# A mixture-of-experts FFN turned round on one Trainium2 core: weights stationary, each expert's 320 lanes moving, tokens scattered to regions in DRAM

## What is computed

```python
x = x + xattn(_layernorm(x), ctx_1024, ctx_1024, Wq, bq, Wk, bk, Wv, bv)
xt = _layernorm(x).reshape(-1, 128)                     # 1024 tokens
top_vals, top_idx = jax.lax.top_k(xt @ gate_w.T, 2)
top_w = jax.nn.softmax(top_vals, axis=-1)
combine = jnp.einsum('tke,tk->te', jax.nn.one_hot(top_idx, 8), top_w)
h = jax.nn.silu(jnp.einsum('td,ehd->eth', xt, w1)) * jnp.einsum('td,ehd->eth', xt, w3)
ye = jnp.einsum('eth,edh->etd', h, w2)                  # w1, w3: 8 x 512 x 128, w2: 8 x 128 x 512
x = x + jnp.einsum('te,etd->td', combine, ye)
```

## Time and profile before

| | us |
|---|---|
| median of three runs | 136.7 |
| lowest and highest | 135.67, 137.67 |
| span of the profiled execution | 132.1 |
| PE busy, POOL busy | 102.9, 84.8 |
| DVE busy, ACT busy | 78.5, 44.1 |

### The profile page before, as it was taken

How to read it: one execution, slowest core, us unless ns; L and a number is a source line. 1 busy time by engine, 2 the same in 40 slices (tenths; PEclk the granted TensorE clock), 3 DMA queues, 4 the chain that set the end, 5 groups by cost and what they waited for, 6 DMA issues and landing times. The chain is left out here.

```text
span 132.1 us, 2609 instructions
## 1 busy us (share of the span) xinstructions
PE 102.9 (78%) x571; PEld 71.5 (54%) x571; DVE 78.5 (59%) x276; ACT 44.1 (33%) x109; POOL 84.8 (64%) x122
## 2 busy tenths in 40 slices
PE   6869976789899279998977897997897979993000
PEld 2245962525355057886866675765675756762000
DVE  0862589897897969996745554563465545632000
ACT  4035877647700013343242033333234033331000
POOL 3387008383975926498769968969979697573630
PEclk9999999869599955999999999999999999999855
DMA  3969999500130002032232322202222323222220
GB/s 108 264 250 424 424 429 404 171 6 0 48 113 18 23 9 39 0 45 24 36 45 40 40 32 27 40 20 40 40 40 40 36 24 40 36 24 20 20 20 0
DMA packets 8119, 11.42 MB, mean 86 GB/s; under 512 B 880, under 2 KB 6896, under 8 KB 7344
## 3 DMA queue, kind: packets, MB, share of 16 engines
q1 hardware_dynamic: 4592, 8.70, 17.7%
q0 software_dynamic: 3520, 2.64, 15.6%
HBM read 8.91 MB, written 2.43 MB: 86 GB/s over the span
## 5 line engine op out<-in xcount | busy, mean ns | idle before, releaser
L381 POOL DMA_INDIRECT out_rows<-y_sb,aid x20 | 31.9, 1595 | 13.9 <-SPq L290 6.4
L523 ACT ACTIVATE hidT<-bank 128x256 f32<-128x256 f32 x40 | 13.5, 382 | 45.6 <-PE bank L997 37.6
L1007 PEld LDWEIGHTS bank<-w_sb,hidT 128*128 128x128 f32 x160 | 19.6, 191 | 7.6 <-issue 7.0
L1007 PE MATMUL bank<-w_sb,hidT 128*128 x160 | 22.4, 283 | 1.6 <-ACT hidT L523 0.9
L360 POOL DMA_INDIRECT xg<-tok_rows,gid x18 | 18.4, 1020 | 7.5 <-DVE slot_w L764 3.4
L974 PE MATMUL bank<-w_hi,xgT 128*128 x40 | 20.1, 503 | 3.0 <-DVE xgT L756 3.0
L910 PE MATMUL bank<-ones 128*128 128x512 bf16 x66 | 20.5, 463 | 1.1 <-DVE ones L544 1.1
L516 ACT ACTIVATE sil<-bank 128x512 f32<-128x512 f32 x20 | 12.1, 603 | 13.9 <-PE bank L976 12.1
L773 DVE TENSOR_TENSOR hid<-bank,sil 128x512 f32<-128x512 f32 x20 | 13.8, 690 | 4.6 <-PE bank L976 2.6
L975 PE MATMUL bank<-w_lo,xgT 128*128 x40 | 16.5, 413 | 0.0
L976 PE MATMUL bank<-w_hi,xgT 128*128 x40 | 16.5, 412 | 0.0
(11 more groups left out here) (120 smaller groups left out, 144.3 us busy)
## 6 DMA issues: line engine op xcount, KB each, us to landing
w_sb<-in_w1T SPq DMA_DIRECT2D x2, 1024.0 KB, 9.9
w_sb<-in_w3T SPq DMA_DIRECT2D x2, 1024.0 KB, 13.6
w_sb<-in_w2T SPq DMA_DIRECT2D x2, 1024.0 KB, 17.2
tok_rows<-tok SPq DMA_DIRECT2D x1, 520.0 KB, 4.4
x_sb<-in_x SPq DMA_DIRECT2D x2, 256.0 KB, 3.2
out_rows<-x SPq DMA_DIRECT2D x2, 256.0 KB, 4.7
ctxT_sb<-in_ctxT SPq DMA_DIRECT2D x1, 480.0 KB, 5.1
out_rows<-y_sb,aid POOLq DMA_INDIRECT x20
```

The costliest lines, as they stand in the source:

```text
L381: nc.gpsimd.indirect_dma_start(out[:, :], bass.IndirectOffsetOnAxis(ap=aid[p][:, 0:1], axis=0), y_sb[p][:, :], None, compute_op=ALU.add).t ...
L523: nc.scalar.activation(hidT[p][:, h * H // 2:(h + 1) * H // 2], ps_hT[h][:, 0:H // 2], ACT.Copy).then_inc(s_hidT, 1)
L1007: last = mm(ps_y[:, 0:D], hidT[p][:, c * P:(c + 1) * P], w2_sb[:, bass.ds(e * H + c * D, D)], start=(c == 0), stop=(c == HC - 1))
```

## The change

**Routing.** Each expert has a region of 1088 rows in a DRAM tensor `expert_rows`; the first 320 (`CAP`) are used by the main part. SP fills these 320 rows of all experts with zeros and row numbers of spare rows, by 16 transfers that stand between w3 and w2 in its queue. The rank product gets the region's start added (`region`), so that the product and sum in `slots` give the row of each pair directly. A row carries the 128 numbers, the token's row in `out` and the weight of the pair; `tok` is there twice, once for each choice (`twin_rows` on ACT). POOL scatters it with 16 indexed DMAs (one for each of 8 batches and 2 choices), and SP loads the regions back, two loads for each expert. The tables of tiles, one-hots, `tok_rows`, all gathers and the copies of row numbers are gone. All low parts are made by DVE, chunks 0 to 3 ahead of the expert loop and the others within it.

**Experts.** The loop is unrolled over 8 experts and 4 chunks of 128 hidden numbers. The weights are stationary and 320 transposed tokens moving: `up` has two split products of three matmuls, `down` one f32 matmul of 320 columns for a chunk; the hidden values come out already turned. The output (`yT`, copied by ACT) is transposed back in three pieces (`turn_out`), weighed by DVE in three pieces and added by POOL in three, with 128, 128 and 64 lanes. Ahead of each expert but the first POOL waits until all adds so far have landed. Experts with more than 320 tokens have further tiles in a loop (`overflow`) that runs a counted number of times, after expert 1; its table is made on DVE ahead of expert 0. `keep_busy` now fills the wait for the scatters.

```diff
+CAP = 320
+LANES = [min(P, CAP - at) for at in range(0, CAP, P)]
...
+            weights(w1_sb, w1T, s_w1)
+            weights(w3_sb, w3T, s_w3)
+
+            sp.wait_ge(s_empty, 2)
+            for e in range(E):
+                for rows, lanes, k in pieces(e):
+                    sp.dma_start(rows, empty_rows[0:lanes, k, :]).then_inc(s_filled, 16)
+            weights(w2_sb, w2T, s_w2)
...
+            for t in range(B):
+                sp.wait_ge(s_put[t], 16 * K2)
+            for e in range(E):
+                for rows, lanes, k in pieces(e):
+                    sp.dma_start(xg[0:lanes, e, k, :], rows).then_inc(s_xg[e], 16)
...
-
             rsqrt(1, 0)
-            low_parts(0, 2)
             rsqrt(1, 1)
-            low_parts(2, 4)
...
-            def gather(p, ids):
-
-                pool.wait_ge(s_rows, 16)
-                nc.gpsimd.indirect_dma_start(
-                    xg[p][:, :], None, tok_rows[:, :],
-                    bass.IndirectOffsetOnAxis(ap=ids, axis=0)).then_inc(s_gat[p], 16)
-
...
-                add_ids(2 * j, 0, 16 * j)
-                gather_next(2 * j + 4, 0)
-                gather_ids(2 * j + 5, 1, 16 * j + 32)
-                add_tile(2 * j, 0)
...
+            pool.wait_ge(s_filled, 32 * E)
+            for g in range(G):
+                pool.wait_ge(s_slot, g + 1)
+                pool.wait_ge(s_pw, 3 * (g + 1))
+                pool.wait_ge(s_twin, g + 1)
+                for t in range(g * TG, (g + 1) * TG):
+                    for c in range(K2):
+                        nc.gpsimd.indirect_dma_start(
+                            expert_rows[:, :], bass.IndirectOffsetOnAxis(ap=slot[:, c, t:t + 1], axis=0),
+                            tok[:, c, t, :], None).then_inc(s_put[t], 16)
...
+            for e in range(E):
+
+                if e:
+                    pool.wait_ge(s_add, 16 * KT * e)
+                if e == OV_AT:
+                    overflow()
+                for k in range(KT):
+                    pool.wait_ge(s_ysb, KT * e + k + 1)
+                    m = LANES[k]
+                    nc.gpsimd.indirect_dma_start(
+                        out[:, :], bass.IndirectOffsetOnAxis(ap=xg[0:m, e, k, D:D + 1].bitcast(U32), axis=0),
+                        y_sb[e % 2][0:m, k, :], None, compute_op=ALU.add).then_inc(s_add, 16)
+            pool.wait_ge(s_add, 16 * KT * E)
...
+            def twin_rows(g):
+                act.wait_ge(s_x2n, (g + 1) * TG)
+                nc.scalar.activation(grp(tok[:, 1], g)[:, :, 0:D], grp(tok[:, 0], g)[:, :, 0:D],
+                                     ACT.Copy).then_inc(s_twin, 1)
...
+            def slots(g):
+
+                dve.wait_ge(s_rank, g + 1)
+                r = ps_rank[g][:, 0:TG * E].unsqueeze(1).broadcast_to([P, K2, TG * E])
+                link(dve_.tensor_tensor(of(pick, g).rearrange("p c t e -> p c (t e)"), r,
+                                        of(oh, g).rearrange("p c t e -> p c (t e)"), ALU.mult))
+                with nc.allow_low_precision("whole numbers below 8192"):
+                    dve_.tensor_reduce(of(slot, g), of(pick, g), AX.X, ALU.add).then_inc(s_slot, 1)
...
+            normalise(1, 0, x1, tok[:, 0], s_x2n)
             norm_stats(1, 1, x1)
+            normalise(1, 1, x1, tok[:, 0], s_x2n)
             dve.wait_ge(s_const, 11)
             top_two(0)
-            normalise(1, 1, x1, x2n, s_x2n)
-            dve.wait_ge(s_rank, 1)
-            link(own_counts(0))
-            link(rank_of(0))
-            link(rank_tile(0))
-            rank_lane(0).then_inc(s_slane, 1)
+            pair_weights(0)
+            slots(0)
             top_two(1)
...
+            pair_weights(1)
+            slots(1)
...
+            def weigh(e):
+
+                dve.wait_ge(s_yr, e + 1)
+                if e > 1:
+                    dve.wait_ge(s_add, 16 * KT * (e - 1))
+                for k, m in enumerate(LANES):
+                    dve_.tensor_scalar(y_sb[e % 2][0:m, k, :], ps_yr[0:m, k * D:(k + 1) * D],
+                                       xg[0:m, e, k, D + 1:D + 2], None, ALU.mult).then_inc(s_ysb, 1)
+
+            overflow_table()
+            low_xgT(0)
+            for e in range(E):
+                if e == OV_AT + 1:
+                    overflow()
+                for c in range(HC):
+                    hidden(HC * e + c)
+                    if c == 2 and e + 1 < E:
+                        low_xgT(e + 1)
+                if e:
+                    weigh(e - 1)
+                if e + 2 < E:
+                    low_parts(2 * (e + 2), 2 * (e + 3))
+            weigh(E - 1)
...
+            for t in range(B):
+                pe.wait_ge(s_put[t], 16 * K2)
+                keep_busy(ps_av, 5)
...
+            def overflow():
+
+                pe.wait_ge(s_ysb, KT * OV_AT)
+                pe.wait_ge(s_yT, OV_AT)
+                pe.wait_ge(s_hid, HC * (OV_AT + 1))
+                with pe.Fori(0, n) as i:
...
-            def turn_hidden(i, p, free=True):
-                pe.wait_ge(s_hid, i + 1)
-                if free:
-                    pe.wait_ge(s_hidT, 2 * i)
...
+            def turn_rows(e):
+                pe.wait_ge(s_xg[e], 32)
+                if e:
+                    pe.wait_ge(s_xgT, e)
+                for k, m in enumerate(LANES):
+                    last = nc.tensor.transpose(ps_xT[:, k * P:k * P + m], xg[0:m, e, k, 0:D], ident[0:m, 0:m])
+                last.then_inc(s_xT, 1)
+
+            def split_product(ps, xT, k, at):
+
+                mm(ps[:, 0:CAP], w_hi[k][:, at], xT[:, 1, :], start=True, stop=False)
+                mm(ps[:, 0:CAP], w_lo[k][:, at], xT[:, 0, :], start=False, stop=False)
+                return mm(ps[:, 0:CAP], w_hi[k][:, at], xT[:, 0, :], start=False, stop=True)
+
+            def up(j):
+                e, c = j // HC, j % HC
+                at = slice(e * H + c * P, e * H + (c + 1) * P)
+                if c == 0:
+                    pe.wait_ge(s_xgT, e + 1)
                     pe.wait_ge(s_wlo, 2 * e + 2)
+                if j > 1:
+                    pe.wait_ge(s_sil, j - 1)
+                split_product(ps_a[j % 2], xgT[e % 2], 0, at).then_inc(s_a, 1)
+                if j > 1:
+                    pe.wait_ge(s_hid, j - 1)
+                split_product(ps_b[j % 2], xgT[e % 2], 1, at).then_inc(s_b, 1)
+
+            def down(j):
+                e, c = j // HC, j % HC
+                if c == 0 and e > 1:
+                    pe.wait_ge(s_yT, e - 1)
+                pe.wait_ge(s_hid, j + 1)
+                at = slice(e * H + c * D, e * H + (c + 1) * D)
+                mm(ps_y[e % 2][:, 0:CAP], w2_sb[:, at], hT[c][:, :], start=(c == 0),
+                   stop=(c == HC - 1)).then_inc(s_d, 1)
+
+            def turn_out(e):
+                pe.wait_ge(s_yT, e + 1)
+                if e:
+                    pe.wait_ge(s_ysb, KT * e)
+                for k, m in enumerate(LANES):
+                    last = nc.tensor.transpose(ps_yr[0:m, k * P:k * P + D], yT[e % 2][:, k * P:k * P + m],
+                                               ident[:, :])
+                last.then_inc(s_yr, 1)
+
             pe.wait_ge(s_w2, 32)
+            turn_rows(0)
+            for j in range(E * HC):
+                e, c = j // HC, j % HC
+                if j == HC * (OV_AT + 1):
+                    overflow()
+                up(j)
+                if j > 1:
+                    down(j - 2)
+                if c == 2 and e + 1 < E:
+                    turn_rows(e + 1)
+                if c == 3 and e:
+                    turn_out(e - 1)
+            down(E * HC - 2)
+            down(E * HC - 1)
+            turn_out(E - 1)
```

More of the change, by code:

```diff
@@ L232, in build, with pieces @@
[L232 to L242 removed]
+        KF = CAP // P
+        def pieces(e):
+            whole, rest = e * REG, e * REG + KF * P
+            return ((expert_rows[whole:rest, :].rearrange("(k p) r -> p k r", p=P), P, slice(0, KF)),
+                    (expert_rows[rest:whole + CAP, :], CAP - KF * P, KF))
@@ L1101 @@
     tokens = inputs["x"].shape[0] * inputs["x"].shape[1]
[L1103 removed]
+    res = nc.dram_tensor("out_rows", (tokens + KT * P, D), F32, kind="ExternalOutput").ap()
     build(nc, *args, res)
```

705 lines of the change are left out of this document (245 added, 460 removed).

## The result

The changed kernel takes 139.56 us (median of 4 runs, 138.34 to 143.40) against 136.50 us of the kernel before beside it: a ratio of 1.026, 95% interval 1.015 to 1.037. Beside other kernels, on another chip, it took 140.15 us (6 runs) against 135.66, 1.033 [1.026, 1.041]. It is slower in both comparisons, by 2.6% and 3.3%; the first interval reaches down to 1.5%, the second stays above 2%. The forecast was 133.8 us and faster. The profiled execution took 138.34 us, its span 136.5, and was the fastest of the four.

A forecast was written before the change was run, and what follows sets the result against it. POOL was taken to set the pace of a tile at 3.35 us, ahead of PE's 2.9. First add at 71.6, expert 1's at 80.0, six periods to 118.9, end 129.2, plus 4.6: 133.8 us; range 128 to 141.5.

The forecast's parts named there:

- Routing and scatters: Before the expert loop: POOL starts at 29.9 us, 16 scatters 1.3 us apart, landed at 52.15, first product at 57.3.
- Rival C: POOL's scatters: a plain scatter costs what a scatter-add costs, interval 1.76 us, whole time 141.1 us; chance 0.22.
- a sign of being wrong: Start of POOL's scatters: the fill transfers would hold the first L317 beyond 31 us.
- One expert on PE: Expert loop on PE: split products 3.53, down 2.2, transposes 0.64 us; 6.37 us per expert, bounds 6.3 and 7.6.
- rival D: PE's products: weight loads are not hidden, 0.19 us per split product, 7.4 us per expert, 138.4 us; chance 0.10.
- Clock and first add: Expert 0: products and turns 11.0 us, low PE clock 2.8, weighing and hand-over 0.5; first add at 71.6 us.
- The overflow test: Ahead of expert 2 on PE: overflow loops run zero times, and PE's drain, registers and branch cost 2.0 us once.
- Rival E: Overflow loop: an expert with over 320 tokens enters it, 26 us more; chance 0.02.
- Adds: POOL between experts: three adds and their landing set a period of 6.48 us, bounds 5.0 and 6.9.
- Rival B: Expert loop: PE sets the pace, adds follow at 1.21 us or the third is short, 129 to 130 us; chance 0.24.
- The time around the span: End of the sum: 4.6 us added to the profiled span to reach the median of the timed runs.

The follow-up runs named there:

- e5_guard: Changed kernel with each engine's overflow loop inside a condition on its count, nothing left out; 136.29 us, 1.005 of the kernel before.
- e6_low_first: Changed kernel without overflow loops and with all of DVE's low parts ahead of the expert loop; 134.94 us, 0.996 of the kernel before.
- e7_busy: Changed kernel without overflow loops and with 11 instead of 5 constant products after each landed batch; 135.72 us, 1.003 of the kernel before.
- e8_best: Changed kernel with overflow loops and PE's waits inside a condition, all low parts ahead of the expert loop, 9 constant products; 133.66 us, 0.983 of the kernel before.
- e1_again: Changed kernel without the overflow loops, run a second time on another chip; 133.87 us, 0.983 of the kernel before.
- e9_busy9: Changed kernel without overflow loops and with 9 instead of 5 constant products after each landed batch; 134.13 us, 0.985 of the kernel before.
- e1_no_pass: Changed kernel with the overflow loops left out on all five engines; 134.05 us, 0.993 of the kernel before.
- e2_drain_only: Changed kernel without overflow loops but with PE's three waits ahead of expert 2 kept; 134.84 us, 0.998 of the kernel before.
- e3_apart: Changed kernel without overflow loops, each expert adding to rows of its own without landing waits (output incomplete); 129.43 us, 0.954 of the kernel before.
- a0_after: The changed kernel unaltered, run again on another chip; 140.15 us, 1.033 of the kernel before.

## Why the prediction was wrong

**Routing and scatters: right.** First L317 at 30.88 us (forecast 29.9: the row numbers were ready at 29.95, 29.75 in the forecast, but POOL started 0.93 us after that and not 0.15), interval mostly 1.26 (1.3), last landed at 52.47 (52.15), first product at 57.02 (57.3). Here are the first and the last of the 16 scatters:

```profile
30.88 1.23 POOL L317 DMA_INDIRECT expert_rows<-tok,slot  x1 [5.03 <-DVE slot L570]
...
50.20 0.95 POOL L317 DMA_INDIRECT expert_rows<-tok,slot  x1 [0.30 <-issue]
```

Rival C, that indexed writing costs 1.60 as in the earlier trace rows, is refuted: the scatter has the gather's price, so the add's 1.56 goes with accumulation. The fills took SP 15.3 us for 16, not 0.5 each; the last was issued at 22.9 us and landed at 29.92, in this execution just as the row numbers were ready, 29.95. That was luck. In eight other profiles the first scatter waits for the fills, in four of them past the 31 us that the forecast had named as a sign of being wrong (e5_guard 31.42, e6_low_first 31.04, e7_busy 31.49, e8_best 32.09), up to about 1.1 us later than the row numbers would have let it:

```profile
31.49 1.23 POOL L306 DMA_INDIRECT expert_rows<-tok,slot  x1 [6.02 <-DMA expert_rows<-empty_rows]
```

**One expert on PE: right in kind.** 6.62 us against 6.37. The weight loads are hidden, and rival D is refuted:

```profile
84.06 0.31 PE L873 MATMUL bank<-xgT,w_hi 128*128 128x320 f32 x1
84.21 0.31 PE L871 MATMUL bank<-xgT,w_hi 128*128 128x320 f32 x1
84.36 0.31 PE L872 MATMUL bank<-xgT,w_lo 128*128 128x320 f32 x1
```

The products follow each other at 0.15 us with a load of 0.20 us for each (the PEld group of L871: 64 loads, 13.1 us). The rule of the Trainium skill, "TensorE: Matmul & The Clock Gate", The mechanism, that such loads overlap running matmuls only where the row groups differ, does not hold here either; an exception that the same section makes, for loads into a background weight buffer, would fit these rows.

**Clock and first add: two errors that nearly cancel.** From 57.27 to 60.86 us 14 products took 3.59 us, where 0.147 each makes 2.06: a loss of 1.5, and 1.5 too by e1_again against e9_busy9 (14.9 and 13.3 us from first product to first add), for which I had 2.8. In e1_no_pass it was 2.6. But with the full clock the way from first product to first add is still 13.3 us (e7_busy, e9_busy9), where I had 11.5: of the 1.8, the weighing and the hand-over to POOL are 0.7, 1.2 us from DVE's start (70.69, L692, to 71.85) and not 0.5. The other 1.1 us I haven't traced to a term. The sum of the two errors, 0.5 us, looks small by luck.

**The overflow test: the step that failed.** "none goes over 320, so every overflow loop runs zero times." The counts were right and the loop's zero was not: its body runs once at a count of zero, as e5_guard shows by adding nothing but the condition. The price I gave for the place, PE's drain of 2.0 us, was the small part: it measured 0.95 to 1.33 us of waiting, and 0.8 us of time (e2_drain_only). The large part is an add and its landing on POOL's chain, 80.29 to 84.44, 4.2 us more of span than forecast, and 3.9 us of time by the condition alone, which itself costs about 0.9. Rival E named this add at the right price for one pass (3.2 and the restart), but asked for an expert over 320 before it ran, and so got 0.02.

**Adds: the right limit, mis-sized by 0.42 us per period.** The pace is three adds and a landing, as forecast, and POOL's idle time ends with the landing. The period is 6.9 and not 6.48:

```profile
95.12 1.43 POOL L344 DMA_INDIRECT out_rows<-xb,xg  x1 [0.30 <-issue]
98.27 1.56 POOL L344 DMA_INDIRECT out_rows<-xb,xg  x1 [1.73 <-DMA out_rows<-xb,xg]
```

The gap between adds is 0.30 and not 0.16 (interval 1.87 twice, +0.2), and an add of 64 rows takes 1.43, hardly less than the 1.56 of 128; from its start to the next group are 3.15 us where I had 2.96 (+0.2). Times six, 2.6 us. Rival B is refuted by the same rows: adds don't follow each other at 1.21.

**The time around the span: 1.8 us, not 4.6.** I compared the span of one execution with the median of others. An execution of the kernel before whose time and span are both known has 134.1 and 132.2 us, and the changed kernel's has 138.34 and 136.5. The profile of before was a quick execution: counted by its span, the forecast should have been 131.0 against about 134. This error of -2.8 hid part of the two above, by luck (4.2 + 2.6 + 0.5 - 0.3 + 0.3 - 0.1 - 2.8 = 4.4, with rounding the 4.5 us from 133.8 to 138.3).

Without the pass the kernel would have been where the step's own logic puts it: 134.0 us in e1_no_pass, 0.2 from the forecast, though by two errors that cancel (the period and the addend). What stays open: the single landing that is up to 0.8 us too long, and what the small edits are worth beside a condition that costs 0.9 us.

## What to carry to other kernels

A loop for the rare case is not free because its count is zero: look in the trace for one pass, and put the loop and the waits ahead of it behind a condition, and count the condition too (about 0.9 us of POOL's chain here). Where indexed adds wait for their landing, the number of adds and landings sets the pace, and the row count hardly does: 64 rows cost 1.43 us and 128 cost 1.56. A transfer that is hidden in one execution can be the last wait in the next, as the fills were. Work saved ahead of such a chain counts only if the first link moves and no later link meets something else.

## What the runs showed of the hardware

- An accumulating indexed transfer that starts while DVE is in low parts (both inputs and the output in SBUF), or up to 0.15 us before, ends 1.3 to 1.5 us behind them (e3_apart: low parts until 80.36, add until 81.80). Mostly it lasts 2.35 to 2.75 us then, but 1.71 where it started near their end (e5_guard: add at 82.76, low parts until 83.02). One that starts 0.36 us ahead of the low parts keeps its 1.56 (a0_after: 94.73 and 95.09). The Trainium skill, "SBUF — State Buffer", Who interferes with whom, says that a DVE instruction with two SBUF inputs contends with a GpSimd instruction that reads SBUF; the adds agree, and the scatters do so only in part: in e6_low_first they take 0.96 us beside the 7.5 us of low parts from 40.92 on, but one beside earlier low parts, at 35.23 us, took 1.50.
- Sixteen fills of a DRAM region from SBUF held SP's queue for 15.3 us, where the sixteen loads back took it 9.2 us. The last fill landed at 29.9 us in the changed kernel and at 31.8 in e8_best.
- PE's clock fell after a pause of 1.25 us behind 17 us of constants (e8_best), and not after one of 0.61 us (e9_busy9); with gaps between the batches of constants ahead it was low from the first products on, or within 1 us of them (a0_after: products 0.147 apart until 57.95 us, 0.267 from 58.14 on), in each kernel with 5 constants and both choices scattered. The granted clock from 58 to 60 us was 0.50 in the changed kernel and 1.00 in e9_busy9, from 60 to 62 us 0.50 in e8_best.
